# New orders for the five queues of an audio tower kernel, bank waits ahead of data waits, and three constants of ScalarE as numbers

## The reference

```
h = x
for i in 0, 1, 2:                         # three state-space layers
    dbc   = h @ W_dbc[i].T                # split into delta (1), B (64), C (64)
    delta = softplus(dbc_delta * W_dt + b_dt)
    state = scan over time of  exp(delta * A) * state + delta * h * B
    h     = sum(state * C) + D * h
    after the first two: mean of each two time steps (375 -> 187 -> 93)
# attention with 8 heads of 8 channels on layernorm(h), weights a polynomial of the score s:
#   0.5 s^2 + s' + const, normalised by their own sum; projection; h += ...
# mixture of 6 experts on layernorm(h), three layers of 64 x 64 each, relu,
#   the best two by a router, weighted by a softmax of their two values; h += ...
out = h                                   # 128 x 93 x 64
```

## Time and profile before

| what | value |
|---|---|
| time of three runs | 648.12, 648.10, 646.14 us, median 648.1 |
| span of the profiled execution | 644.8 us; 3.3 below the median of the runs |
| PE busy | 572.2 us, 89% (weight loads 302.5, beside it) |
| DVE busy | 540.6 us, 84% |
| ACT busy | 525.0 us, 81% |
| POOL busy | 423.5 us, 66% |
| pm, 128 activations on ACT | 107.4 us |
| landing of a swap (x_B<-x_B), from issue | 2.2 us (median) |

### The profile page before, as it was taken

The page is one execution under the profiler, slowest core; times in us unless marked ns, Lnnn a source line. Parts: engine busy times, 40 slices in busy tenths (PEclk is TensorE's granted clock), DMA queues, the critical chain, the costliest instruction groups (busy, mean ns, idle before and its releaser), DMA issues.

```text
span 644.8 us, 22886 instructions
## 1 busy us (share of the span) xinstructions
PE 572.2 (89%) x9531; PEld 302.5 (47%) x9531; DVE 540.6 (84%) x1019; ACT 525.0 (81%) x1044; POOL 423.5 (66%) x549
## 2 busy tenths in 40 slices
PE   3777778999999999999999999999999999999972
PEld 2333234545455555455445455455545545545431
DVE  5898999999899899989898999999898987764441
ACT  1345668989899999998898998999999888888761
POOL 7758899788867677768567766767686755423110
PEclk9998879999999999999999999999999999999998
DMA  3432222221220213230211212220221001000001
GB/s 78 83 82 63 65 59 59 61 52 31 52 48 20 56 43 77 47 74 14 69 31 45 55 44 61 58 47 15 68 49 29 5 8 31 17 14 14 2 14 29
DMA packets 77575, 28.52 MB, mean 44 GB/s; under 512 B 69271, under 2 KB 77463, under 8 KB 77463
## 3 DMA queue, kind: packets, MB, share of 16 engines
q1 hardware_dynamic: 71290, 25.92, 17.6%
q10 hardware_dynamic: 6173, 1.05, 0.9%
HBM read 13.25 MB, written 3.05 MB: 25 GB/s over the span
## 4 chain that ended last, share of the span: by engine, by line
PE 44%; ACT 19%; DVE 17%; POOL 9%; issue 5%; DMA 2%; ACTq 2%; SPq 1%; POOLq 0%; DVEq 0%
PE ring L1274 7%; PE ring L1353 5%; ACT pm L1057 5%; PE ring L1366 4%; PE ring L1461 4%; DVE ring L1714 3%; PE ring L1260 3%; PE ring L1432 2%; PE ring L1441 2%; ACT hid L1100 2%; PE ring L1229 2%; PE ring L1249 2%; PE ring L1336 1%; PE ring L1412 1%; DVE carry_C L1710 1%
## 5 line engine op out<-in xcount | busy, mean ns | idle before, releaser
L1057 ACT ACTIVATE pm<-ring,two_col 93x744 f32<-93x744 f32 x128 | 107.4, 873 | 10.0 <-PE ring L1353 9.0
L1353 PE MATMUL ring<-q_exp,qk 32*93 32x372 f32 x512 | 56.4, 507 | 7.7 <-ACT ln_rows_a L1021 1.1
L1821 DVE TENSOR_TENSOR hidw<-hid,ring 128x744 f32<-128x744 f32 x48 | 44.3, 922 | 19.1 <-PE ring L1422 11.5
L911 POOL TENSOR_TENSOR q_exp<-qk,mask_q 128x1488 f32<-128x1488 f32 x16 | 42.9, 2683 | 22.2 <-DVE qk L1772 22.2
L1366 PE MATMUL ring<-pm,v 97*32 97x93 f32 x2048 | 53.7, 245 | 1.2 <-ACT pm L1057 0.4
L1100 ACT ACTIVATE hid<-ring,b_col 128x372 f32<-128x372 f32 x96 | 49.3, 568 | 1.5 <-PE ring L1441 0.9
L1366 PEld LDWEIGHTS ring<-pm,v 97*32 97x32 f32 x2048 | 42.4, 109 | 15.3 <-ACT pm L1057 3.4
L1107 ACT ACTIVATE hid<-ring,b_col 128x744 f32<-128x744 f32 x48 | 42.2, 879 | 8.9 <-PE ring L1432 6.4
L1432 PE MATMUL ring<-hid,w 64*64 64x372 f32 x384 | 40.3, 489 | 3.2 <-ACT hid L1100 2.7
L896 POOL TENSOR_TENSOR base_C<-base_C,carry_C 128x744 f32<-128x744 f32 x16 | 28.5, 1781 | 20.1 <-DVE carry_C L1723 9.5
L1441 PE MATMUL ring<-nrm_f,w 64*64 64x372 f32 x384 | 40.0, 486 | 0.2
(11 more groups left out here) (368 smaller groups left out, 1755.4 us busy)
## 6 DMA issues: line engine op xcount, KB each, us to landing
xin_A<-in_x_dram SPq DMA_DIRECT2D x62, 93.0 KB
xin_B<-in_x_dram SPq DMA_DIRECT2D x62, 93.0 KB
x_A<-x_A SPq DMA_DIRECT2D x32, 93.0 KB, 2.4
x_B<-x_B SPq DMA_DIRECT2D x32, 93.0 KB, 2.2
x_C<-x_C SPq DMA_DIRECT2D x32, 93.0 KB, 2.2
out_dram<-osb SPq DMA_DIRECT2D x15, 186.0 KB
x_D<-x_D SPq DMA_DIRECT2D x32, 46.5 KB, 2.2
w<-in_L_ffn_expert_w_dram SPq DMA_DIRECT2D x6, 48.0 KB
```

What stands on the lines that cost most here:

```text
L1057: a.activation(pm[q % 2][h][0:TOUT].rearrange("m a j n -> m a (j n)"), out_of(f"att.s{q}{h}", g)[0:TOUT, :, 0:COLS], ACT.Square, bias=two_ ...
L1353: ins = mm(o[h][0:TOUT, b, 0:COLS], qk[r:r + 32, 1, q * TOUT:(q + 1) * TOUT], q_exp[r:r + 32, q].rearrange("p j n -> p (j n)"), start=True ...
L1821: tt(hidw[k][:], hid2[:], out_of(f"ffn.g_{k}", g)[:, :, 0:COLS], ALU.mult).then_inc(me, 1)
```

## The change

All five lists in ORDER are written anew. They hold the same steps in another order. Counted by places: of PE's 1000 entries 701 are at the same place and none has moved by more than 10; of ACT's 917, 484 and 11; of DVE's 670, 209 and 39; of POOL's 277, 162 and 5; of SP's 115, 33 and 5. PE's entries have new banks. 789 of PE's entries end in "!": for these do() calls bank() for the step's jobs before the step's own function, so that the waits for the place stand ahead of the waits for the data (need() then leaves them out the second time). Three constants of ACT, the tiles two_col, ln_col and eps_col with their memsets on DVE, are gone; the activations have the number itself as bias.

```diff
-        two_col = sb("two_col", [P, 1])
-        ln_col = sb("ln_col", [P, 1])
-        eps_col = sb("eps_col", [P, 1])
...
-            "pe": ("prep.w0:0/0 A.xT:0/2 prep.w1:0/1 A.row:0/0 B.xT:0/2 B.row:0/2 prep.qkvp:0/0 A.z:0/2 B.dpre:0/4 "
-                    "B.z:0/6 A.dpre:0/2 prep.w2:0/0 B.s:0/2 B.b:0/6 B.xT:1/0 A.s:0/4 B.c:0/2 B.row:1/0 A.b:0/4 B.dpre:1/6 "
...
-                    "ffn.g_1:15/0 ffn.h1_2:15/4 ffn.h2_2:15/4 ffn.g_2:15/0 ffn.oT:14/6 ffn.o:15/0 ffn.oT:15/0"),
-            "act": ("A.x:0 prep.l3:0 B.x:0 A.row:0 prep.exp:0 B.row:0 prep.l5:0 B.exp:0 A.exp:0 B.ln:0 A.ln:0 prep.l2:0 "
-                    "B.x:1 B.decay:0 B.row:1 B.exp:1 B.ln:1 A.decay:0 B.decay:1 A.x:1 C.row:0 A.row:1 C.exp:0 C.ln:0 "
...
+            "pe": ("prep.w0:0/6 prep.w2:0/7 B.xT:0/0 B.row:0/3 A.xT:0/0! A.row:0/0 B.z:0/4 A.z:0/6 B.dpre:0/2 A.dpre:0/4 "
+                    "B.s:0/2! prep.w1:0/4! prep.qkvp:0/7! B.b:0/0! B.xT:1/2! B.row:1/4 A.b:0/2! B.c:0/4! A.s:0/6! B.dpre:1/0 "
...
+                    "ffn.lg:15/6 ffn.h2_2:14/2 ffn.h1_0:15/0! ffn.h1_1:15/4! ffn.g_2:14/0! ffn.h2_0:15/2 ffn.h1_2:15/6! "
+                    "ffn.o:14/1 ffn.gT:15/0 ffn.h2_1:15/4 ffn.g_0:15/2 ffn.g_1:15/2! ffn.oT:14/6! ffn.h2_2:15/4! ffn.g_2:15/2! "
+                    "ffn.o:15/6 ffn.oT:15/6"),
+            "act": ("prep.l5:0 prep.l2:0 B.x:0 B.row:0 A.x:0 A.row:0 prep.exp:0 B.exp:0 B.ln:0 A.exp:0 prep.l3:0 A.ln:0 A.decay:0 "
+                    "B.decay:0 B.x:1 B.row:1 B.exp:1 B.ln:1 A.x:1 A.row:1 B.decay:1 C.row:0 C.exp:0 C.ln:0 C.decay:0 A.exp:1 "
+                    "B.x:2 A.ln:1 B.row:2 A.decay:1 B.exp:2 B.ln:2 A.x:2 B.decay:2 D.row:0 D.exp:0 A.row:2 D.ln:0 C.row:1 "
...
+                    "ffn.rh:15 ffn.hid1_2:14 ffn.prexp:15 ffn.out:13 ffn.hid2_2:14 ffn.hid1_0:15 ffn.topexp:15 ffn.topln:15 "
+                    "ffn.toprec:15 ffn.hid1_1:15 ffn.hid2_0:15 ffn.gateT:15 ffn.hid1_2:15 ffn.hid2_1:15 ffn.out:14 ffn.hid2_2:15 "
+                    "ffn.out:15"),
+            "dve": ("prep.back:0 prep.w0:0 prep.w2:0 B.quad:0 prep.mean:0 A.quad:0 prep.dec:0 B.most:0 A.most:0 B.base:0 "
+                    "B.based:0 B.vin:0 prep.w1:0 prep.qkvp:0 B.scan:0 A.vin:0 B.carry:0 A.base:0 A.scan:0 A.based:0 A.carry:0 "
+                    "B.quad:1 B.vin:1 B.most:1 prep.late:0 B.scan:1 B.base:1 B.carry:1 B.based:1 prep.cen:0 C.vin:0 C.quad:0 "
...
+            "sp": ("prep.l0:0 B.load:0 A.load:0 prep.l1:0 B.swap:0 A.swap:0 B.load:1 A.load:1 B.swap:1 prep.l4:0 B.load:2 "
...
+        FIRST = {tuple(entry.split("/")[0].split(":")) for entry in ORDER["pe"].split() if entry[-1] == "!"}
...
-            BANK |= {(job, int(g_)): int(b) for job, b in zip(PAIRED.get(w_, (w_,)), banks_.split(","))}
+            BANK |= {(job, int(g_)): int(b) for job, b in zip(PAIRED.get(w_, (w_,)), banks_.rstrip("!").split(","))}
...
-                    a.activation(ln_rows[w][:], out_of(f"{u}.var", g)[:, 0, 0:TOUT], ACT.Ln, bias=eps_col[:]).then_inc(me, 1)
+                    a.activation(ln_rows[w][:], out_of(f"{u}.var", g)[:, 0, 0:TOUT], ACT.Ln, bias=LN_EPS).then_inc(me, 1)
...
-                    a.activation(qk_norm[:], qk_norm[:], ACT.Exp, bias=ln_col[:], scale=-0.5).then_inc(me, 1)
+                    a.activation(qk_norm[:], qk_norm[:], ACT.Exp, bias=12.0 * LN2, scale=-0.5).then_inc(me, 1)
...
-                                 bias=two_col[0:TOUT], scale=0.5 ** 0.5).then_inc(me, 1)
+                                 bias=2.0, scale=0.5 ** 0.5).then_inc(me, 1)
...
             def do(g, u, s):
+                if (f"{u}.{s}", str(g)) in FIRST:
+                    for job in PAIRED.get(f"{u}.{s}", (f"{u}.{s}",)):
+                        bank(g, job)
                 {"att": attention, "ffn": experts, "prep": prepare}.get(u, ssm)(g, u, s)
...
-            for t_, val in ((zero_col, 0.0), (clamp_col, CLAMP), (under_col, -UNDERFLOW),
-                            (two_col, 2.0), (ln_col, 12.0 * LN2), (eps_col, LN_EPS)):
+            for t_, val in ((zero_col, 0.0), (clamp_col, CLAMP), (under_col, -UNDERFLOW)):
...
-            consts = 13 + 6 + 14 + NX + len(cleared) + 4
+            consts = 13 + 6 + 11 + NX + len(cleared) + 4
```

## The result

The changed kernel takes 657.75 us (median of 4 runs, 656.07 to 659.61) where the kernel before, run beside it, takes 647.12: a ratio of 1.0165, 95% interval 1.0144 to 1.0187, 10.7 us slower. The forecast was 647.0 in a range of 638.5 to 654.5. The profiled execution spans 655.7 us and itself took 657.4.

A forecast was written before the change was run, and what follows sets the result against it. TensorE (PE) was taken as the bound between 100 and 620 us, VectorE (DVE) setting the pace between 20 and 100. Sum: 648.1 + 7.0 - 3.3 - 1.5 - 2.0 - 1.3 = 647.0 us, range 638.5 to 654.5.

The forecast's parts named there:

- Start: First groups: ACT's twelve DMA issues ahead of its first copy delay x_B and the first exponential; 7.0 us lost, bounds 0 to 9.2.
- The rule of the Trainium skill: Start: weighed against that term; by it the twelve moved issues would be nearly free and the sum 7.0 lower.
- Constants: ACT's activations with numbers as bias: 82 to 92 ns shorter each, 3.3 us gained, bounds 0 and 14.9.
- The three memsets gone from DVE are 0.06 us each ... nothing: DVE, before PE has anything to do: removing the memsets of the constants' tiles was priced at nothing.
- The rest of the lists and the banks: Outside the start, PE steps move under one place on average: gain 1.3 us, bounds -4 (a loss) and 12.
- PE's idle time between 100 and 620 us: Sign for the forecast: PE's idle time in the middle stretch should be several us below 25.2.
- Waits: PE steps with two waits, order turned by the marks: 29 x 0.06, taken as 1.5 us gained, bounds -1.0 and 2.5.
- End: Last group: out:14 is copied earlier, so its store holds up out:15 less; 2.0 us gained, bounds 0 and 2.7.
- PE takes over as the last wait: End: the last group's own work, ready at 634.8, rather than the store of out:14, becomes the last wait.
- less than 6 us apart: Sign for the end: the last two osb copies this close, with the second released by PE.
- Rival (b): Whole kernel slower: the start's 9.2 us delay reaches the end, ACT's shorter squares gain nothing; 653.8 us, chance 0.22.

The follow-up runs named there:

- before_best: The kernel before with the three constants as numbers, a spare tile keeping the old addresses, and the waits for banks first: 641.3 us, ratio 0.9907.
- old_200: As old_start, but the lists change from those of before to the new ones at about 200 us instead of 89: 638.8 us, ratio 0.9857.
- old_start: pad_swap with the start of all five lists taken from before up to about 89 us, new lists from there: 643.1 us, ratio 0.9920.
- pad_swap: The kernel after with a spare tile of 96 bytes (old addresses) and C.swap:7 ahead of B.load:9 in SP's list: 650.2 us, ratio 1.0038.
- old_start_early: old_start with ACT's twelve issues of prep.l5 and prep.l2 ahead of its first copy: 650.3 us, ratio 1.0036.
- late_issues: The kernel after with ACT's prep.l5 and prep.l2 moved back to where they stood before, other lists new: 659.5 us, ratio 1.0183.
- consts_pad: consts plus an unused spare tile of 96 bytes per partition, so every later tile has its old address: 645.1 us, ratio 0.9950.
- swap_first: The kernel after with one exchange in SP's list, C.swap:7 ahead of B.load:9: 651.7 us, ratio 1.0061.
- before_first: The kernel before with waits for the bank ahead of those for data at the 789 marked steps: 645.9 us, ratio 0.9968.
- old_200_tail: old_200 with the end of before as well, PE's last 14 entries and ACT's last 9: 639.5 us, ratio 0.9876.
- consts: The kernel before with only ACT's three constants as numbers, their tiles and memsets gone: 650.6 us, ratio 1.0054.
- pad_late: consts with the 96-byte spare tile behind x, so only the work tiles from soft on have old addresses: 650.6 us, ratio 1.0040.
- consts_last: The kernel before, constants still in tiles but allocated last, so everything from rank on lies 96 bytes lower: 653.7 us, ratio 1.0102.
- after_pad: The kernel after with a spare tile of 96 bytes, so the old addresses: 654.1 us, ratio 1.0095.

## Why the prediction was wrong

Going from before to after through before_best, old_200, old_start and pad_swap, the steps are: constants and marks -6.0, new lists behind 200 us with the end -3.2, new lists between 89 and 200 us with the seam +4.1, start +7.6, addresses and stall together +8.2. The sum is the measured 10.7, as it must be for differences taken one after the other; it doesn't prove the names given to them, and the border between the 4.1 and the 7.6 lies where the lists were cut.

- **Start: right in size and in mechanism, with luck in the parts.** Forecast +7.0, measured +7.6 (pad_swap against old_start), and the times of its instants were within 0.5 us, some by errors that cancel. That an issue holds ACT's queue is shown by old_start_early: 8.3 us later at x_B's copy, 7.5 at the end. The rule of the Trainium skill weighed there ("DMA: Bandwidth & Descriptors", section "Issuing engines are not separate DMA queues") calls the time for starting a DMA usually small beside the DMA itself. Here twelve of them, ahead of a first step, were not small: 8.2 us. (The shortest of the twelve took 0.55 us, not 0.60.) How much of the delay in after is the issues' and how much the lists' isn't separated: late_issues left six of them where they hold up the decays. Nor did I look at which load lands first.
- **Constants: right in size.** Forecast -3.3, measured -3.2 (consts_pad), so of the 14.9 us of ACT's time 3.2 were on the path. pm fell by 90 ns and qk_norm by 94. "ScalarE: Activation LUTs" of the Trainium skill, section "What ACT_TABLE_LOAD costs", has about 93 ns for a pointer operand; the trace agrees.
- **"The three memsets gone from DVE are 0.06 us each ... nothing": the step that failed first.** I priced the instructions of the removed tiles and not the tiles. Without them xin and x lie 96 bytes lower, and that costs 6.7 us in the orders of before, 4.5 in after, for a term put at nothing.
- **"The rest of the lists and the banks": the other step that failed.** I took a gain of 1.3, and a loss of 4 at most, as if a list were a cloud of small moves. One place of SP's list cost 3.7 us at the old addresses and 6.7 at the new: a load directly behind a store and ahead of a swap for which PE was waiting. I had read SP's list for the first 45 us only. PE's idle time between 100 and 620 us, which was to fall, rose to 31.7; in swap_first it is 520.00 - 492.74 = 27.3. The cut at 89 us showed 4.1 more, of which the seam may be a part. Only behind 200 us do the new lists gain, 3.2 with the end.
- **Waits: right mechanism, too small.** Forecast -1.5, measured -2.1 on the old order and -4.6 on the new. The price of 0.06 us held (0.104 - 0.042). I had counted 29 turned waits in the trace of before, and before_first turns 27; in the new order it is 62, beyond the bound of 2.5 us.
- **End: right by the traces.** From gateT:15's end to the end of the last copy 11.6 us in before and 9.8 in after, -1.8 for -2.0; by the times of old_200 and old_200_tail it is 1.2, not clear of noise. ACT's timeline of after, against the earlier trace rows:

```profile
638.21 0.48 ACT L1096 ACTIVATE gateT<-ring 128x372 bf16<-128x372 bf16 x1 [1.18 <-PE ring L1433]
...
641.14 0.59 ACT L1104 ACTIVATE osb<-ring 93x512 f32<-93x512 f32 x1
...
647.92 0.59 ACT L1104 ACTIVATE osb<-ring 93x512 f32<-93x512 f32 x1 [4.91 <-DMA out_dram<-osb]
```

That PE takes over as the last wait holds in old_200, whose last copy has "5.17 <-PE ring L1446". In after it is a tie: by the semaphores oT:15 ends at 647.81 and the store of out:14, which took 6.08 us to land instead of 5.25, at 647.84. My test for it ("less than 6 us apart") was wrong, though: the two copies are 6.78 apart, because the first moved as well; my own instants, 628.2 and 634.8, were 6.6 apart.

Rival (b) had the sign, and a like size (653.8), for another reason: it needed the constants to gain nothing. With addresses and stall mended (pad_swap) the kernel is 2.5 us slower than before, where the forecast had it 1.1 faster; those 3.6 us are of the size of the 4.1 at 89 to 200 us. With either one mended (654.1, 651.7) it would have been inside the stated range.

## What to carry to other kernels

Before a small tile is removed or added, look at what is allocated behind it; a spare tile that keeps the targets of the DMAs in place tells the two effects apart. In a written-out order, read each in-order queue for its issues: what long issue, above all one behind a large store, stands ahead of a short one that somebody waits for. When an experiment moves something out of the way, look in its trace whether it now stands in another's. And take a bundle apart before it is thrown away or kept: the constants of this one gained 3.2 us, the order of the waits 2.1 to 4.6, the new lists behind 200 us with the end 3.2, in a whole that lost 10.7.

## What the runs showed of the hardware

- The same 71,290 packets of the hardware queue took 113 us of all 16 engines with xin and x at their old place, 119 to 121 with both 96 bytes lower (consts, pad_late, after, consts_last), and 113 to 115 with 32 bytes higher or 64 lower. The four issues of a load took 4.93 us on average in after, 4.68 in after_pad. The longer packets are those of 256 bytes, 74.6 us in consts and 66.6 in consts_pad; the packets of the swaps, taken together, are not longer.
- DMA issues hold the queue of the engine that makes them: twelve small ones on ACT ran from 14.23 to 22.46 us in old_start_early, and the copy behind them was 8.3 us later than in old_start.
- A load's four issues directly behind a store of 186 KB took 8.62 us in after and 7.48 in before; ordinary ones about 4.5. Where the load came 8 us behind the store (after, 217.31) they took 4.50. In swap_first the swap behind the store took 2.52 for its two issues, and the load behind it 4.67.
- After 5.3 us without work PE came back mostly at the lower of its two levels, 1.2 GHz: the mean granted clock of the 5 us from 270 on was 0.57, where before had 1.00 in the same stretch.
- With two waits ahead of a weight load of PE, the load started 0.104 us after the release where the separate wait was the last, and 0.042 where the one that rides on the load was.
